# A routed expert layer on one core: where the register of a block's expert is loaded, and one semaphore per batch of result rows

## The reference

```
x = x + attention(layernorm(x))             # causal, 16 heads, 4 groups of keys and values, rotary
x = x + cross_attention(layernorm(x), ctx)  # 16 heads over 375 context rows of 128
x = x + experts(layernorm(x))

experts(xt):
  scores = sigmoid(xt @ gate.T)             # 8 experts
  sel    = top 2 of scores + expert_bias
  for each (token, chosen expert e): row = (xt[token] * score).bfloat16
      h  = silu(row @ w1[e].T) * (row @ w3[e].T)        # 512 -> 256
      out[token] += h @ w2[e].T                         # 256 -> 512
  out += (silu(xt @ shared_w1.T) * (xt @ shared_w3.T)) @ shared_w2.T
```

## Time and profile before

| what | value |
|---|---|
| median of 3 runs | 651.95 us (650.67 to 653.23) |
| the profiled execution, its own time | 654.79 us |
| its span, first to last instruction | 653.0 us |
| mean granted clock of PE over the span | 0.938 |
| PE busy, share of the span | 570.5 us, 87% |
| PEld busy | 445.7 us, 68% |
| DVE busy | 391.6 us, 60% |
| ACT busy | 290.8 us, 45% |
| POOL busy | 295.4 us, 45% |

### The profile page before, as it was taken

One profiled execution on the slowest core, in us unless ns is written; L12 is line 12 of the kernel. 1 busy time (PEld: TensorE's weight loads), 2 busy tenths in 40 slices (PEclk: granted clock), 3 DMA queues, 4 the chain that ended last, 5 costly groups with the idle time before them and its releaser, 6 DMA issues. The chain is left out here.

```text
span 653.0 us, 9766 instructions
## 1 busy us (share of the span) xinstructions
PE 570.5 (87%) x3435; PEld 445.7 (68%) x3440; DVE 391.6 (60%) x908; ACT 290.8 (45%) x660; POOL 295.4 (45%) x290
## 2 busy tenths in 40 slices
PE   2767998998989699999999999999999599888862
PEld 1544676665757489888888888888888399653320
DVE  6553777686575666557565565646565476446551
ACT  3132542633635376547763476536764041113320
POOL 0508642643833366505963178603973107305540
PEclk9978997998979899999999999999999958999995
DMA  8854545665633059215433262424200182492443
GB/s 267 216 181 124 184 168 175 216 196 177 228 119 120 1 162 270 34 41 156 125 81 80 85 193 46 73 57 161 66 1 0 37 355 71 110 179 82 130 130 112
DMA packets 52978, 85.00 MB, mean 130 GB/s; under 512 B 25698, under 2 KB 34612, under 8 KB 52036
## 3 DMA queue, kind: packets, MB, share of 16 engines
q1 hardware_dynamic: 50276, 72.47, 35.3%
q0 software_dynamic: 2656, 11.91, 8.1%
HBM read 63.20 MB, written 30.09 MB: 143 GB/s over the span
## 5 line engine op out<-in xcount | busy, mean ns | idle before, releaser
L1448 POOL TENSOR_TENSOR xprob<-xprob,erec 128x375 f32<-128x375 f32 x112 | 90.3, 814 | 136.3 <-DVE erec L1227 136.0
L915 ACT ACTIVATE xprob<-s_ps,nmax 128x375 f32<-128x375 f32 x112 | 64.2, 574 | 59.8 <-DVE nmax L1222 56.9
L1222 DVE TENSOR_REDUCE nmax<-s_ps 128x1 f32<-128x375 f32 x112 | 59.6, 538 | 0.0
L59 PE MATMUL k_ps<-ow,ctx_hl 128*112 128x512 f32 x128 | 52.5, 410 | 2.8 <-DVE ctx_hl L1217 2.1
L61 PE MATMUL k_ps<-ow,ctx_hl 128*112 128x512 f32 x128 | 50.4, 394 | 0.0
L1217 DVE TENSOR_TENSOR ctx_hl<-k_ps,ctx_hl 128x448 fp32r<-128x448 f32 x32 | 20.0, 625 | 50.6 <-ACT ctx_hl L910 50.6
L1441 POOL TENSOR_TENSOR prob<-prob,rec 112x1792 f32<-112x1792 f32 x8 | 25.5, 3187 | 54.7 <-DVE rec L1163 54.7
L60 PE MATMUL k_ps<-ow,ctx_hl 128*112 128x512 f32 x128 | 50.2, 392 | 0.0
L1197 DVE TENSOR_TENSOR pt_hl<-f_ps,pt_hl 125x512 fp32r<-125x512 f32 (+1 forms) x67 | 41.7, 623 | 11.1 <-ACT pt_hl L887 10.0
L59 PE MATMUL s_ps<-kvt,qt_hl 128*128 128x376 f32 x112 | 44.9, 401 | 2.0 <-ACT xprob L915 1.0
L1684 POOL DMA_INDIRECT done_dram<-o_sb,to x28 | 27.1, 968 | 43.1 <-DVE o_sb L1958 41.1
(11 more groups left out here) (239 smaller groups left out, 1535.3 us busy)
## 6 DMA issues: line engine op xcount, KB each, us to landing
ow_raw<-ow_dram SPq DMA_DIRECT2D x16, 512.0 KB, 3.6
w<-w_dram SPq DMA_DIRECT2D x6, 1024.0 KB, 10.8
raw_b<-in_raw SPq DMA_DIRECT2D x8, 640.0 KB, 5.1
raw_m<-in_raw SPq DMA_DIRECT2D x8, 576.0 KB, 4.1
raw_q<-in_raw SPq DMA_DIRECT2D x8, 512.0 KB, 6.5
ow_dram<-bw_sb SPq DMA_DIRECT2D x8, 512.0 KB, 5.8
qw_raw<-aw_dram SPq DMA_DIRECT2D x16, 256.0 KB, 3.5
w_dram<-in_w POOLq DMA_DIRECT2D x8, 512.0 KB, 5.4
```

Of the source, the lines that this page charges most:

```text
L59: pe.matmul(out, a_hl[0], b_hl[0], start=start, stop=False, skip_group_check=True)
L915: act.activation(xprob[z][:, 0:L], s_bank(n, k)[:, 0:L], ACT.Exp, bias=nmax[:, z:z + 1], accum_out=esum[:, z:z + 1]).then_inc(xexp_done, 1)
L1222: dve.tensor_reduce(nmax[:, z:z + 1], s_bank(n, k)[:, 0:L], X, ALU.max, negate=True).then_inc(xmax_done, 1)
L1448: pool.tensor_tensor(xprob[z][:, 0:L], xprob[z][:, 0:L], erec[:, z:z + 1].broadcast_to([128, L]), ALU.mult).then_inc(xp_ready, 1)
```

## The change

PE's order: the register load leaves `up` and becomes `owner_of(g)`. Two of them stand before the first block, and the one for block g + 2 stands right behind `up(g + 1)`, before `turn_hidden(g)`. The wait for all eight shared additions (`d_added`) leaves the front of the blocks and becomes a third wait of the first `turn_hidden`. The semaphores of the result rows, one a half with 4 DMAs each, become one for each of the four places in a half, counted up by the second half; a gather waits for the load of its own batch. The number of loads, products, DMAs and copies stays.

```diff
--- before.py
+++ after.py
@@ -1602,7 +1602,7 @@
         up_done, up_silu, hid_done, o_done, o_copied = (
             sem("up_done"), sem("up_silu"), sem("hid_done"), sem("eo_done"), sem("eo_copied"))
         hid_turned, hid_copied = sem("hid_turned"), sem("hid_copied")
-        got_loaded = [sem(f"got_loaded{h}") for h in range(HALVES)]
+        got_loaded = [sem(f"got_loaded{s}") for s in range(HALF)]
         c_done, y_ready, y_stored = sem("c_done"), sem("y_ready"), [sem(f"y_stored{z}") for z in range(2)]
 
         def put_by(g):
@@ -1639,7 +1639,7 @@
                     for s in range(HALF):
                         b = HALF * h + s
                         src = done_dram[h][0:SPARE].rearrange("(r b t) c -> b t r c", r=TOP2, b=HALF)
-                        sp.dma_start(got[:, b], src[s]).then_inc(got_loaded[h], 16)
+                        sp.dma_start(got[:, b], src[s]).then_inc(got_loaded[s], 16)
 
                 def store(b):
                     sp.wait_ge(y_ready, b + 1)
@@ -1742,11 +1742,13 @@
                                  start=(m == 0), stop=(m == HC - 1))
                     mm.then_inc(d_done, 1)
 
-                def up(g):
+                def owner_of(g):
                     h, j = g // BLOCKS, g % BLOCKS
                     if j == 0:
                         pe.wait_ge(own_ready, h + 1)
-                    e = pe.value_load(own_e[0:1, h, j:j + 1], min_val=0, max_val=EXPERTS - 1)
+                    return pe.value_load(own_e[0:1, h, j:j + 1], min_val=0, max_val=EXPERTS - 1)
+
+                def up(g, e):
                     if g % CHUNK == 0:
                         pe.wait_ge(xg_loaded[g // CHUNK], 16)
                     r = slice(g % CHUNK * 128, (g % CHUNK + 1) * 128)
@@ -1754,11 +1756,12 @@
                     for k in range(KC):
                         mm = pe.matmul(b_ps[g % 2][:, :], xg[:, g // CHUNK, k, r], w13[:, e, :, k, :], start=(k == 0), stop=(k == KC - 1))
                     mm.then_inc(up_done, 1)
-                    return e
 
                 def turn_hidden(g):
                     pe.wait_ge(hid_done, g + 1)
                     wait(pe, hid_copied, g)
+                    if g == 0:
+                        pe.wait_ge(d_added, B)
                     bank = h_ps[:, :].bitcast(BF16)
                     for m in range(HC):
                         mm = pe.transpose(bank[:, m * 128:(m + 1) * 128], hid[g % 2][:, m * 128:(m + 1) * 128], ident_bf[:, :])
@@ -1772,7 +1775,7 @@
                     mm.then_inc(o_done, 1)
 
                 def gather(b):
-                    pe.wait_ge(got_loaded[b // HALF], 16 * HALF)
+                    pe.wait_ge(got_loaded[b % HALF], 16 * (b // HALF + 1))
                     wait(pe, y_ready, b)
                     for r in range(TOP2):
                         mm = pe.matmul(c_ps[0:T, :], ident_bf[0:T, 0:T], got[:, b, r, :], start=(r == 0), stop=(r == TOP2 - 1))
@@ -1794,12 +1797,14 @@
                 for b in range(B):
                     shared_down(b)
                 pe.wait_ge(tri_ready, 3)
-                pe.wait_ge(d_added, B)
                 pe.wait_ge(w_loaded, 16 * 6)
-                owner = [up(0)]
+                owner = [owner_of(0), owner_of(1)]
+                up(0, owner[0])
                 for g in range(ALL):
                     if g + 1 < ALL:
-                        owner.append(up(g + 1))
+                        up(g + 1, owner[g + 1])
+                    if g + 2 < ALL:
+                        owner.append(owner_of(g + 2))
                     turn_hidden(g)
                     if g:
                         down(g - 1, owner[g - 1])
```

## The result

| | before | after | ratio of the times, 95% interval |
|---|---|---|---|
| first set, median | 652.59 us (4 runs) | 645.82 us | 0.9888 [0.9842, 0.9935] |
| second set | 650.75 us (29 runs) | 644.53 us (6 runs) | 0.9903 [0.9871, 0.9935] |
| profiled execution, first set | 654.79 us, span 653.0 | 644.5 us, span 642.7 | |

The kernel is faster by 1.1% (0.65 to 1.6), some 7 us in the first set and 6 in the second; 645.4 was predicted. The median of after in the first set is over four executions, one of which was disturbed (1380.32 us); it is left out of the ratio, and the other three took 643.59 to 647.13.

A forecast was written before the change was run, and what follows sets the result against it. The block period follows the count of PE's sequencer instructions, not PE's arithmetic. Gains 2.4 + 1.3 + 0.5 + 2.4 = 6.6 us give 648.2 from the profiled 654.79, or 645.4 from the median 651.95; range 643.0 to 649.0.

The forecast's parts named there:

- The start, 2.4: First blocks: moving the wait gains 1.75 us, loading for block 2 before the first transpose 0.65, together 2.4 us earlier.
- The loop, 0: Loop over 28 blocks: the load only changes its place, the period stays 1.67 us, nothing gained or lost.
- 0.07 a block, 1.9 us: Loop, bound not taken into the sum: the gain were each register load as short as the shortest.
- The first gather, 1.3: Gather of batch 0: with its own semaphore it no longer waits for all four loads; 1.3 us, possibly down to 0.
- (e): First gather's stall was an accident of the profiled execution, gathers behind gain nothing: 4.8 us, 647.2; 0.70 together with the forecast.
- The gathers behind it, 0.5: Three gathers after the first: a register load before the gather covers the wait for the addition; 0.5 us, bounds 0 and 0.65.
- (b): Register load dearer at its new place by 0.05 to 0.2 us, 26 loads give back 1.3 to 5.2 us; chance 0.13.
- The end, 2.4: Gather of batch 4 waits only for its own load, starting at 640.2 instead of 642.56: 2.4 us gained.
- the other case: Last four gathers: at full PE clock they take 0.64 instead of 1.10, 1.8 us more; kept in the range's lower part.
- (a): Loop: sequencer has unseen slack, period falls from 1.67 towards 1.41, 6.8 us more, 638.6; chance 0.05.
- (c): Loop: register load waits for the products in front, period grows by 0.63 to 2.3, 661.7; chance 0.04.
- (d): Start doesn't move because something else holds the first block: 4.2 us gained, 647.7; chance 0.08.

The follow-up runs named there:

- e2: Kernel before with only the wait for the shared additions moved to the first transpose; ratio to before 0.9984 [0.9961, 1.0007].
- e1: Changed kernel with only the new order of register loads, wait and semaphores as in the kernel before; ratio to before 1.0007 [0.9982, 1.0031].
- e11: Changed kernel, with SP storing 6 times 0.9 MB from SBUF to spare DRAM beside the first half's blocks; ratio to before 0.9968 [0.9943, 0.9994].
- e0: The changed kernel itself, run once more in the second set; ratio to before 0.9903 [0.9871, 0.9935].
- e3: Kernel before with only the separate semaphores for each batch's place in the result-row loads; ratio to before 0.995 [0.9928, 0.9972].
- e7: Changed kernel with 30 unused products behind the last block, to keep PE busy in the last gap; ratio to before 0.9898 [0.9865, 0.993].
- e4: Changed kernel with every register load from block 3 on made twice, 25 loads more; ratio to before 1.0157 [1.0103, 1.021].
- e8: Changed kernel without the bounds assertion of each loaded expert number; ratio to before 0.9904 [0.9872, 0.9937].

## Why the prediction was right, and where it was not

**The start, 2.4: right.** 1.83 + 0.69 = 2.52. Both mechanisms were seen alone, the wait in e2 (1.95), the order in e1 (0.69). What e1 adds is that without the first the second gains nothing: with the wait in front, the second register load costs 0.74 there.

**The loop, 0: its mechanism right, its size off by 0.78, and the division behind it wrong.** The working divides 616.25 - 586.19 by 18. Those are the products of blocks 4 and 21, 17 apart, so the period of before was 1.77 us over them and not 1.67. Rightly divided, the period was some 0.1 above the sum of the sequencer's instructions, 1.6 to 1.7, and that would have asked what the excess is. 0.06 us a block of it is the loads' own duration above 302 ns. The view by line shows the loads of the blocks for before, 585.4 to 615.2, and for after, 578.8 to 606.0:

```profile
L1749 PEldq TENSOR_LOAD <-own_e x18: 297/314/537, 585.4 to 615.2; - x18
```

```profile
L1749 PEldq TENSOR_LOAD <-own_e x17: 297/302/539, 578.8 to 606.0; - x17
```

Single durations between up(3) and up(20) add up to 6.15 us over 17 loads before and 5.38 after. The difference, 0.77, is the 0.78 that the stage gained. One load of after, at 582.0, took 539 ns, as one of before did at 590.4 (537); the other 16 took 297 to 308. At its new place the load falls between the packets of the puts, not on them: two windows that hold a load of 302 ns each, at 604.3 and 606.0, have a DMA share of 0.00. The bound "0.07 a block, 1.9 us" of the prediction held it. That a DMA can do this to a load is shown by e11; that the puts do it in the kernel before is the reading of two traces. Full DMA engines alone do not: the load of after at 607.7 took 302 ns beside the loads of the result rows, at a share of 1.12.

The Trainium skill, in "DMA: Bandwidth & Descriptors", section "Latency and other measured facts", has a tensor_load at about 600 ns at least. At the new place the trace disagrees too, 302 ns in the median; a load of one value above 600 is seen only beside other transfers (870 to 952 in e11, 668 to 803 for three of the last four loads in e0).

**The first gather, 1.3: right.** up(20) to up(22) went from 5.12 to 3.86. Whether the stall was an accident of one execution, (e), is answered by the two kernels that keep the old semaphore: 5.11 in e1, 4.54 in e2. It is there each time, with 0.6 us of play. Each is one execution.

**The gathers behind it, 0.5: this step failed**, the stage lost 0.32. The term took a "register load of 0.65 us" at that place at its usual price. The load did come to stand between the products and the gather and did cover the wait for the addition: the gather of batch 3 starts at 616.98, 0.6 us behind the end of the addition that frees its bank (before: 0.1). But there the load runs beside SP's stores of the first results and is dearer. Loads from 613 to 620 us, after:

```profile
L1749 PEldq TENSOR_LOAD <-own_e x4: 431/717/792, 613.1 to 619.5; - x4
```

Windows that hold the first two of them, and ahead of these one in the blocks and the one at 607.7 (last columns: DMA share, GB/s):

```profile
604.30:604.60 0.30, 0.30 (x3) 0.16 (x2) 0.30 (x1) 0.00 (x0) 0.30 (x1) 1.00 0.00 0
...
607.70:608.00 0.30, 0.30 (x3) 0.18 (x2) 0.30 (x1) 0.00 (x0) 0.23 (x1) 1.00 1.12 430
...
613.10:613.80 0.70, 0.70 (x5) 0.29 (x3) 0.70 (x3) 0.00 (x0) 0.00 (x0) 1.00 0.74 199
615.30:616.10 0.80, 0.80 (x5) 0.29 (x3) 0.80 (x2) 0.00 (x0) 0.03 (x1) 1.00 0.92 266
```

These four took 675, 792, 431 and 759 ns; the loads of before in this stretch (from 620.5 on) took 669, 300, 302, 332 and 350. So rival (b) was true for four loads and for no other: 1.45 us above 302 in all, 1.01 more than before, whose loads had 0.44; the miss is 0.82. Whether the order does this is best read over both gather stages, up(20) to up(27), since the old order puts the boundary up(22) elsewhere: order alone 15.17 us (e1) against 14.83 (before), order beside the new semaphores 13.88 (e0) against 13.35 (e3). So it costs 0.3 to 0.5 us there by these single executions, and e3's loads in this stretch took 297 to 382 ns. The slow loads came back in e0, e1, e7 and e11, which have the same order. Why stores of results slow a load and the loads of result rows do not stays open.

**The end, 2.4: right**, 2.26, and 2.49 in e3. The clock stayed at its lower level for the gathers, 0.50 from 632.3 on, as I took it, behind 7.53 us of idle; e7 shows what the other case is worth, 1.46.

**The median.** 645.4 was the sum taken from 651.95; the sets gave 645.82 and 644.53. The two errors of the sum, 0.78 gained in the loop and 0.82 missed behind the first gather, cancel; that the sum hit so closely is luck, that start, first gather and end did is not. The rivals: (a) refuted by e4; (b) holds for four loads; (c) refuted by e1; (d) by e2; (e) refuted for the stall, right on the gathers behind it.

## What to carry to other kernels

Where a loop's instructions take their addresses from registers, add up the sequencer's instructions before those of the engine: a register load with the work on its value was 0.67 us of each block and all of it on the path, and moving it off the front of a block gave 0.8 us in 17 blocks, as far as two traces show because it then missed the puts. Taking it out of the loop gave PE its own pace there, but 2.2 of the 4.2 us so gained were lost again where the loads were put. A wait holds everything behind it in its queue, so it belongs directly in front of the instruction that needs it, and a group of transfers whose parts are used one by one should count on one semaphore each; here these two edits were most of the gain, and the reordering that came with them was worth nothing alone. When a gain is read from stages, look ahead of the first stage too, if the edit put work there. When an interval is divided by a count, name both ends by their block first.

## What the hardware showed that I had not expected

- A register load from SBUF took 297 to 308 ns in 16 of 17 blocks of the kernel after, and 870 to 952 beside stores from SBUF that filled the DMA engines (share 1.03, 409 GB/s). Beside the loads of result rows, at a share of 1.12, it took 302.
- Its price rises with the number of values: 302 ns for one, 547 for two, 1715 for 14.
- A weight load that waits for a semaphore holds the register load behind it: the one at 582.3 started when the weight load was released, and so did the one of e2 at 575.96. A load in front of it runs in the wait's shadow.
- Behind the hole at 594.5 to 597.6 in a stretch of full clock, the granted clock was 0.58 for 3.5 us (e8), so a hole costs more than its length.
